# Order of the first transfers in a ternary-weight convolution: image 0, weights, images 1 to 3 on one queue

## The reference, cut to what matters

```python
x = x + conv(_gn(x), wq, padding=1) + bias     # x: 32 x 128 x 56 x 56, fp32; 3x3 filters, 128 -> 128 channels

def _gn(v, G=32, eps=1e-05):                   # over groups of 4 channels of one image
    g = v.reshape(B_, G, C_ // G, H_, W_)
    return ((g - mean(g)) / sqrt(var(g) + eps)).reshape(v.shape)

def _quantize(weight, Wp, Wn):
    max_val = max(abs(weight))                 # over the whole weight tensor
    delta = 0.05 * max(abs(weight / max_val))
    tern = where(w_norm > delta, 1, where(w_norm < -delta, -1, 0))
    return where(tern > 0, Wp[0] * tern, where(tern < 0, Wn[0] * tern, tern))
```

## Time and profile before

| what | value |
|---|---|
| time before, median of 3 runs | 559.02 us (558.83 to 559.25) |
| the profiled execution: its own time | 559.39 us |
| the profiled execution: span of the trace | 557.8 us |
| busy: PE / DVE / ACT / POOL | 524.3 / 539.1 / 508.0 / 140.0 us |
| granted TensorE clock, share of full | 0.995 |
| HBM traffic | 273 GB/s over the span |

### The profile page before, as it was taken

One profiled execution on the slowest core, in us unless ns is written; L12 is line 12 of the kernel. 1 busy time (PEld: TensorE's weight loads), 2 busy tenths in 40 slices (PEclk: granted clock), 3 DMA queues, 4 the chain that ended last, 5 costly groups with the idle time before them and its releaser, 6 DMA issues. The chain is left out here.

```text
span 557.8 us, 9357 instructions
## 1 busy us (share of the span) xinstructions
PE 524.3 (94%) x3233; PEld 317.1 (57%) x3233; DVE 539.1 (97%) x507; ACT 508.0 (91%) x485; POOL 140.0 (25%) x105
## 2 busy tenths in 40 slices
PE   1798999999999999999999999999999999999994
PEld 0554555665556556655565565556556565565552
DVE  3998999999999999999999999999999999999994
ACT  4999999999999999999999999999999999999850
POOL 2020333211333321233332123333213333211320
PEclk9999999999999999999999999999999999999998
DMA  7539899999999999999999999999999999998755
GB/s 283 220 116 240 251 294 289 283 258 265 360 264 322 300 282 270 298 317 278 298 320 280 264 326 284 287 280 326 299 283 281 295 322 288 299 267 214 160 161 223
DMA packets 27960, 152.63 MB, mean 274 GB/s; under 512 B 3488, under 2 KB 3488, under 8 KB 27936
## 3 DMA queue, kind: packets, MB, share of 16 engines
q1 hardware_dynamic: 18576, 102.77, 48.2%
q0 software_dynamic: 8784, 48.98, 45.1%
q10 hardware_dynamic: 576, 0.59, 0.3%
HBM read 100.94 MB, written 51.38 MB: 273 GB/s over the span
## 5 line engine op out<-in xcount | busy, mean ns | idle before, releaser
L790 PE MATMUL odd_rows<-parts,w_lhsT 128*128 128x392 f16 (+1 forms) x1536 | 262.7, 326 | 6.7 <-DVE parts L622 6.3
L790 PE MATMUL even_rows<-parts,w_lhsT 128*128 128x392 f16 (+1 forms) x1536 | 262.2, 326 | 3.1 <-DVE parts L622 1.9
L622 DVE SCALAR_TENSOR_TENSOR parts<-plane,norm_scale,parts 128x1568 f16<-128x1568 f32 x127 | 232.7, 1836 | 1.7 <-ACT parts L399 1.7
L790 PEld LDWEIGHTS even_rows<-parts,w_lhsT 128*128 128x128 f16 x1536 | 148.6, 97 | 106.6 <-DVE parts L622 2.7
L399 ACT ACTIVATE parts<-plane,norm_scale 128x1568 f16<-128x1568 f32 x127 | 199.8, 1596 | 9.0 <-ACT plane L439 5.2
L790 PEld LDWEIGHTS odd_rows<-parts,w_lhsT 128*128 128x128 f16 x1536 | 146.6, 99 | 104.8 <-DVE parts L622 8.6
L336 POOL TENSOR_TENSOR plane<-x 128x1512 f32<-128x1512 f32 x31 | 85.9, 2771 | 372.4 <-DVE parts L622 372.4
L445 ACT ACTIVATE junk<-x,negmean 128x3136 f16<-128x3136 f32 x32 | 92.9, 2904 | 0.1
L405 ACT ACTIVATE junk<-x 128x3136 f16<-128x3136 f32 x31 | 87.0, 2805 | 0.0
L637 DVE SCALAR_TENSOR_TENSOR y<-even_rows,out_scale,d_sb 128x784 f32<-128x784 f32 x62 | 63.3, 1021 | 0.0
L637 DVE SCALAR_TENSOR_TENSOR y<-odd_rows,out_scale,c_sb 128x784 f32<-128x784 f32 x62 | 63.2, 1019 | 0.0
(11 more groups left out here) (66 smaller groups left out, 108.3 us busy)
## 6 DMA issues: line engine op xcount, KB each, us to landing
x<-in_x_dram SPq DMA_DIRECT2D x64, 784.0 KB, 11.2
out_dram<-y SPq DMA_DIRECT2D x63, 784.0 KB, 5.9
y<-in_x_dram POOLq DMA_DIRECT2D x61, 784.0 KB, 11.6
out_dram<-y SPq DMA_DIRECT2D x2, 392.0 KB, 5.2
y<-in_L_conv_weight_dram ACTq DMA_DIRECT2D x1, 576.0 KB, 6.7
wp_sb<-in_L_conv_Wp_dram ACTq DMA_DIRECT2D x1, 0.5 KB, 7.5
wn_sb<-in_L_conv_Wn_dram ACTq DMA_DIRECT2D x1, 0.5 KB, 8.3
bias_sb<-in_L_conv_bias_dram ACTq DMA_DIRECT2D x1, 0.5 KB, 8.0
```

The costliest lines, as they stand in the source:

```text
L622: nc.vector.scalar_tensor_tensor(part(img, j, LO), plane[j][:], norm_scale[:, b_slice(img)], part(img, j, HI), ALU.mult, ALU.subtract).the ...
L790: ins = nc.tensor.matmul(product_ps(odd, b, b + 1)[:, 0, r0 - b * BANK_ROWS:r1 - b * BANK_ROWS, :], w_lhsT[:, prod, kh, :], part(img, prod ...
```

## The change

SyncE issues the weights where it used to wait for them, on its own queue, between image 0 and image 1; ScalarE no longer issues them.

```diff
@@ sync, emit, first slot @@
                         for img in (nxt, far, third, fourth):
                             if img.buf != nxt.buf or img is nxt:
                                 if p == 0 and img is far:
-                                    sp.wait_ge(w_loaded, 16)
+                                    sp.dma_start(w_raw, weight.rearrange("o i h w -> o (i h w)")).then_inc(w_loaded, 16)
                                 load(img, 0, first=img is nxt)
                                 load(img, 1, first=img is nxt)
@@ scalar @@
-            act.dma_start(w_raw, weight.rearrange("o i h w -> o (i h w)")).then_inc(w_loaded, 16)
             act.dma_start(wp_sb[:], wp.rearrange("(a b) -> a b", a=1).broadcast_to([P, 1])).then_inc(scalars_loaded, 16)
```

## The result

The changed kernel takes **561.0 us** (median of 8 runs, 560.52 to 561.03) against 559.02 us in as many runs of the kernel before (558.6 to 559.66). The ratio is 1.0035, with a 95% interval of 1.0025 to 1.0044: slower by 2.0 us, which is 0.35% and clear of the interval. The forecast was 559.7 us, the range ended at 560.5.

A forecast was written before the change was run, and what follows sets the result against it. VectorE, busy for 97% of 557.8 us, was taken as the bound, so early losses show whole. Weights at 9.6 plus a 7.65 us chain put the variance at 17.25 instead of 16.56: 559.02 + 0.69 = 559.7 us; range 558.9 to 560.5.

The forecast's parts named there:

- the small transfers' share: Start of kernel: the three scalar transfers sharing the engines with image 0 and the weights cost 0.5 us, as before.
- the middle value 9.6: Weights' landing in the new order, in us, taken midway between 9.3 by bytes and 9.8 with the scalars' 0.5.
- the lower bound: Earliest landing of the weights: issue at 0.94 + 4.6 for a lone half + 1.9 + 1.4 = 8.84 us.
- The other, 9.3: Weights' landing by bytes without scalars: first half at 6.0, second at 7.9, weights at 9.3 us.
- the predicted 0.69: Variance of image 0 on VectorE: taken at 17.25 instead of 16.56 us, a loss of 0.69 us.
- Rival A: Start of ScalarE's queue: scalars alternating with image 0 delay the weights to 10.3 us, giving 560.4 us; chance 0.22.
- the second payment in front of the weights: Weights' landing: the slowest engine pays for the scalars beside image 0 and again before the weights, which land at 10.3.
- B: Start of kernel: one queue alone starts faster, weights' bytes moved at 7.2 us, giving 557.3 us; chance 0.05.
- C: Shared queue: engines still take weights' packets along with image 0's, landing near 7.64, time stays 559.0 us; chance 0.05.
- the two chains: Before image 0's variance: weight chain on VectorE reaches it at 17.25 us, image chain over ScalarE and TensorE at 16.61.
- nothing absorbs it: From 22 us on VectorE has no room, so a loss in the first 22 us appears whole at the end.
- the removed wait is worth nothing: SyncE's wait before loading images 1 to 3: removing it gains nothing and loses nothing; image 1 already had 2.2 us cover.

The follow-up runs named there:

- the old order with late small transfers: Kernel before with weights alone on ScalarE's queue, no wait, and wp, wn, bias on SyncE's queue behind image 1's first half: 558.83 us, ratio 0.9993.
- the run with late small transfers: Changed kernel with wp, wn and bias moved to SyncE's queue behind the first half of image 1: 559.38 us, ratio 0.9999.
- the turned program: Changed kernel with wp, wn, bias behind image 1's first half, plane D before the weights' maxima, mean before their turn: 558.53 us, ratio 0.9984.

## Why the prediction was right and wrong

**Wrong: the landing of the weights, and in it one term.** The step that failed is the small transfers' share: 0.5 us in either order, taken at half by way of the middle value 9.6. Against the run that has the same order with the small transfers out of the way, they cost 10.56 - 8.91 = 1.65 us. Of the two sums by bytes the lower bound was right: bytes and the start of a lone half gave 8.84, and that run has 8.91. The other, 9.3, was 0.4 us too late, for the most part because it began from a first half that had itself been slowed. Where the working went astray was the sentence that the same transfers take the same time in any order. In the kernel before, the weights stood in front of the small transfers on ScalarE's queue (they landed at 7.64, wp at 1.38 + 7.5 = 8.9), and mainly the second half of image 0 met those: against the old order with late small transfers it is 0.88 us late (9.84 and 8.96), the first half and the weights 0.37. The move put wp at the head of that queue, beside the first half, and the weights behind all of it. The cost of a packet of 4 bytes is not in its 4 bytes: beside wp the other transfers move at about half their rate (188 to 226 GB/s, where 420 flow without it).

At the variance the 1.48 us are 0.71 for the order and 1.65 - 0.88 = 0.77 for the small transfers, which cost more in the new place than in the old one. The 0.77 is about the whole miss. That the 0.71 lies beside the predicted 0.69 is partly luck, since the prediction had small transfers in both of its landings.

**Rival A** named the place (the scalars now alternate with image 0 from the first packet), but not the second payment in front of the weights: against the run with late small transfers the readers of the two halves and of the weights start 1.52, 1.59 and 1.65 us later, so nearly all is paid at the first half. Its price of 1.0 us in all was too small as well: 10.3 and 560.4, against 10.5 and 561.0. I gave it 0.22; the point against it, that three transfers of 0.5 KB are not more work in another place, is what the runs deny. Rivals B and C did not occur. The Trainium skill's rule beside B (DMA: Bandwidth & Descriptors, section "Anatomy of one DMA — SWDGE (gpsimd) path": 2.0 us for a transfer, here taken once for the three, then bytes at 436 GB/s) gave 7.9 for the weights; with nothing in the way they land at 8.9, so on this queue it is 1.0 us short, and with the small transfers in the way 2.6.

**Right: the two chains.** The wait of 0.85 us in front of plane D and that of 0.42 in front of the variance are gone. From the start of L529 to L599 there are 18.04 - 10.56 = 7.48 us, where 7.65 was added up; back to back, an instruction starts some hundredths before the one in front of it ends (L581 at 11.83, where L529 ends at 11.91). The mean starts 1.74 us after L529 (1.95 predicted), because it has to wait for L744, and image 0's head start is lost there, in VectorE's and TensorE's order; the turned program shows it (15.63 against 16.39). The sum of the terms: +0.69 predicted, +0.96 for the later landing, -0.17 for the shorter chain, which is the 1.48 measured at L599.

**Right: nothing absorbs it, and the removed wait is worth nothing.** 1.48 us at L599 are 1.48 at the first product and 1.5 at the end of the span, and the order alone, with the wait kept, can't be told from the change (ratios 1.0026 and 1.0035, whose intervals overlap). Both hold for this order: in the old order, taking the wait out made the kernel slower (1.0024).

**Partly open.** The medians lie 2.0 us apart and the traces 1.5. That the kernel before was profiled in an execution 0.37 us above its median covers most of the difference; no second trace of it was compared. Executions of one kernel can also differ behind the first slot: two other traces have the 1.2 us wait at the variance of image 1 that neither of these two has.

## What to carry to other kernels

When a transfer is moved between queues, ask what becomes first on the queue that it leaves: the small loads that stood behind it now run beside the transfers on which the start of the kernel hangs. Put loads of a few bytes per partition from one small region of memory where nothing urgent is in flight: not beside an urgent transfer, and not directly behind one in the same queue, where they cost 1.7 us in one run and nothing in another. Price them by a run, not by their bytes. Before an order is called free, compare it with the old one after the same disturbance has been taken out of both. And a transfer that comes earlier was worth something here only when the engines' written order asked for it before the transfer that was put behind it.

## What the runs showed of the hardware that was not expected

- Three transfers of 128 numbers of 4 bytes each (144 packets each in the trace), from 4-byte or 512-byte regions, delay 2.2 MB beside them by 1.65 us (weights at 10.56 instead of 8.91). When they read columns of the weights instead, at addresses 4,608 bytes apart, they delay them by nothing (8.87).
- One such transfer, wp, which reads a single number 128 times, does it alone (10.63); the second one of the kind, right behind the first, adds almost nothing, in either order of the two (10.56 and, in one execution, 10.54). Beside the bias alone the rate from 4 to 6 us is 314 and 308 GB/s, and the first sum starts at 6.26 instead of 5.68; the weights are at 9.54, but a trace with no small transfer beside them had 9.56, so 0.6 us is not a sure price for them.
- Beside wp the slices move 188 to 226 GB/s, at 4 to 6 us in two kernels and at 7 to 9 us in a third; with wp in the same queue behind image 0, it is 107 and 82 GB/s.
- The first half of image 0 (784 KB), with no other queue beside it, lands 4.6 us after its issue at the very start of the kernel, as a half does at 28.84 us in the middle of it.
